# Attention stage of a four-layer block: when a finished group of heads is copied, transposed and divided, and where its products stand

## What is computed

```python
def _L1_ffn_ref(x, attn_norm_w, ffn_norm_w, wq, wk, wv, wo, gate_w, expert_w):
    # _gqa: 16 query heads, 4 key heads, head width 8
    attn = jnp.einsum('bqhd,bkhd->bhqk', q, k) * scale
    attn = jnp.where(causal, attn, jnp.float32(-jnp.inf))
    attn = jax.nn.softmax(attn, axis=-1)
    out = jnp.einsum('bhqk,bkhd->bqhd', attn, v).reshape(B, S, C)
    ...
    h = x + _gqa(_rmsnorm(x, attn_norm_w), wq, wk, wv, wo)
    out = h + _moe(_rmsnorm(h, ffn_norm_w), gate_w, expert_w)   # top 2 of 8 experts
    return out
```

## Time and profile before

| | |
|---|---|
| median of 3 runs | 1509.01 us (1503.67 to 1511.28) |
| the profiled execution | 1498.92 us |
| its span in the trace | 1497.5 us |
| mean granted TensorE clock | 0.892 of full |
| attention steps | from about 846 us to 1464 us of the span |

### The profile page before, as it was taken

The page is one execution under the profiler, slowest core; times in us unless marked ns, Lnnn a source line. Parts: engine busy times, 40 slices in busy tenths (PEclk is TensorE's granted clock), DMA queues, the critical chain, the costliest instruction groups (busy, mean ns, idle before and its releaser), DMA issues. The chain is left out here.

```text
span 1497.5 us, 18717 instructions
## 1 busy us (share of the span) xinstructions
PE 1171.4 (78%) x5568; PEld 540.4 (36%) x5568; DVE 1141.2 (76%) x3062; ACT 734.8 (49%) x1603; POOL 681.7 (46%) x823
## 2 busy tenths in 40 slices
PE   3514997899998877766677778898989889989885
PEld 1202454555545443323221323333333333333222
DVE  5888645757988897888978786787888778778217
ACT  4645684255443344232310457656566456645772
POOL 7433673465777678467550122124421532153312
PEclk9855997999999998887866788999999999999998
DMA  3000104321111100012221301002020302000001
GB/s 110 0 1 0 48 1 109 81 74 64 43 43 43 28 29 0 0 24 46 47 43 39 67 1 37 27 14 39 1 37 4 49 1 37 4 1 1 4 1 56
DMA packets 33682, 47.02 MB, mean 31 GB/s; under 512 B 5023, under 2 KB 18207, under 8 KB 33279
## 3 DMA queue, kind: packets, MB, share of 16 engines
q1 hardware_dynamic: 30990, 43.84, 13.1%
q10 hardware_dynamic: 2592, 2.00, 0.5%
HBM read 39.14 MB, written 6.68 MB: 31 GB/s over the span
## 5 line engine op out<-in xcount | busy, mean ns | idle before, releaser
L1691 ACT ACTIVATE RB<-PS 128x512 f32<-128x512 f32 (+3 forms) x768 | 327.8, 496 | 220.5 <-PE PS L673 216.9
L621 PE MATMUL PS<-B 96*128 96x512 bf16 (+3 forms) x768 | 256.4, 356 | 67.6 <-DVE B L1258 24.1
L1964 POOL TENSOR_SCALAR_AFFINE_SELECT RB<-RB 128x512 f32<-128x512 f32 x128 | 81.3, 635 | 411.5 <-ACT RB L1691 411.5
L1189 DVE CUSTOM_DVE_ANT_0 PS<-PS,w_msk 128x128 f32<-128x128 f32 (+3 forms) x512 | 243.6, 503 | 29.3 <-PE PS L621 28.9
L673 PE MATMUL PS<-B 96*128 96x512 bf16 (+3 forms) x768 | 242.7, 338 | 23.1 <-ACT RB L1691 21.4
L1192 DVE TENSOR_REDUCE SS<-PS 128x1 f32<-128x512 f32 x256 | 175.3, 685 | 44.3 <-PE PS L621 43.2
L690 PE MATMUL PS<-RB,B 128*32 128x512 f32 (+3 forms) x1536 | 171.4, 519 | 14.0 <-ACT RB L1698 14.0
L621 PEld LDWEIGHTS PS<-B 96*128 96x128 bf16 x768 | 77.5, 102 | 218.5 <-DVE SS L1189 67.3
L1870 POOL TENSOR_TENSOR RB<-RB,B 128x512 f32<-128x512 f32 x64 | 82.4, 1290 | 89.0 <-DVE RB L1017 66.8
L673 PEld LDWEIGHTS PS<-B 96*128 96x128 bf16 x768 | 75.6, 100 | 103.5 <-ACT RB L1691 63.9
L1536 ACT ACTIVATE RB<-PS 128x512 f32<-128x512 f32 x72 | 42.8, 596 | 128.4 <-PE PS L438 128.3
(11 more groups left out here) (261 smaller groups left out, 2239.2 us busy)
## 6 DMA issues: line engine op xcount, KB each, us to landing
B<-scrW SPq DMA_DIRECT2D x128, 128.0 KB, 3.0
B<-scrQ SPq DMA_DIRECT2D x72, 128.0 KB
scrQ<-B SPq DMA_DIRECT2D x6, 384.0 KB, 3.0
B<-scrK SPq DMA_DIRECT2D x36, 64.0 KB
X<-in_x SPq DMA_DIRECT2D x8, 256.0 KB, 8.7
out_dram<-X SPq DMA_DIRECT2D x7, 256.0 KB, 3.2
B<-in_w SPq DMA_DIRECT2D x3, 576.0 KB, 5.4
B<-in_zeros SPq DMA_DIRECT2D x9, 128.0 KB
```

What stands on the lines that cost most here:

```text
L621: pe.matmul(p[:, 0:w], qs[u % 3][:, h, 128 * i:128 * i + 128], keys_of(u, h)[:, 512 * c:512 * c + w], start=True, stop=True).then_inc(s["m ...
L1189: ins = dve.tensor_tensor_reduce(p, p, msk[:, 512 - w:512], 1.0, LOWEST, ALU.add, ALU.max, MX[:, u % 2, i, h, c:c + 1])
L1691: act.activation(RB[:, 4 * (step % 3) + z, 0:w], bank(bank_of["score", step, z])[:, 0:w], ACT.Exp).then_inc(s["ex2"], 1)
L1964: pool.affine_select(out=pb, in_=pb, compare_op=ALU.is_ge, fill=0.0, base=0, pattern=[[0, 4], [1, 128]], channel_multiplier=-1).then_inc(s ...
```

## The change

Four things are issued at other places; nothing is added or removed.

- ACT: `sums` stands after the four exps of step E+2, not between the second and third exp of step E+3.
- PE: `heads_2` stays in step E+3, but in front of `product_2(E+1)` instead of behind it.
- DVE: `divide` stands after the four maxima of step E+3, not between the second and third maximum of step E+4.
- PE: the `post_h` slices of every step stand in front of both (behind the scores, ahead of `heads_2` and `product_2`), not at the end of the step. `pass_f(3, k)` of the first unit stays last.

```diff
@@ tensor_program
-                if 0 <= step - PLAG < 192:
-                    product_2(step - PLAG)
+                for g, k in post_slices(step):
+                    post_h(step, g, k)
                 if 0 <= step - PLAG - 1 < 192:
                     n, kt = STEPS[step - PLAG - 1]
                     if kt == 4 * GROUPS[n][2] + 3:
                         heads_2(n)
+                if 0 <= step - PLAG < 192:
+                    product_2(step - PLAG)
                 if u < 7 and r == 20:
                     guard_1(u + 1)
                 for k in late_slices(step):
                     pass_f(3, k, lambda: next_1(step))
-                for g, k in post_slices(step):
-                    post_h(step, g, k)
@@ vector_program
-                for v, n in ahead[0:2]:
+                for v, n in ahead:
                     highest(v, n)
-                if 0 <= step - PLAG - 2 < 192:
-                    n, kt = STEPS[step - PLAG - 2]
+                if 0 <= step - PLAG - 1 < 192:
+                    n, kt = STEPS[step - PLAG - 1]
                     if kt == 4 * GROUPS[n][2] + 3:
                         divide(n)
-                for v, n in ahead[2:]:
-                    highest(v, n)
@@ scalar_program
                 if step < 192:
-                    exps(step, 0)
-                    exps(step, 1)
-                if 0 <= step - PLAG - 1 < 192:
-                    n, kt = STEPS[step - PLAG - 1]
+                    for z in range(4):
+                        exps(step, z)
+                if 0 <= step - PLAG < 192:
+                    n, kt = STEPS[step - PLAG]
                     if kt == 4 * GROUPS[n][2] + 3:
-                        sums(n, step - PLAG - 1)
-                if step < 192:
-                    exps(step, 2)
-                    exps(step, 3)
+                        sums(n, step - PLAG)
```

## The result

The changed kernel took **1454.12 us** (median of 4 runs, 1450.34 to 1458.79) against 1507.42 us for the kernel before (4 runs, 1503.67 to 1511.28). The ratio on record is 0.968, 95% interval 0.9648 to 0.9712; the two medians alone give 0.9646, just outside it. I had forecast 1480 and a range down to 1464. The sign and the places were right; the gain is larger than the range allowed.

A forecast was written before the change was run, and what follows sets the result against it. PE was taken as nearest to the bound, DVE right behind, each waiting in turn at group ends. Terms 4 + 22 + 3 = 29 us off the 1509.0 us median gave 1480 us; the range ran from 1464 to 1505.

The forecast's parts named there:

- Bound and mechanism: Attention stage: PE nearest to a bound, DVE right behind; at group ends they wait in turn, which reordering gives back.
- copy (and transposes): Group ends: copy moved ahead of two exps on ACT, transposes ahead of the product; 4 us won, bounds 0 and 14.
- division: Group ends: division falls into DVE's idle time, so PE's raw blocks stop waiting for it; 22 us won.
- post slices: 28 expert steps: matmuls start a product earlier, mostly off the path; 3 us won, upper bound 5.5, lower a loss.
- worked case: One group end: fourth score at 1096.1 instead of 1095.99, next step's first block 0.1 us earlier.
- The copy holds the exps: Rival: ACT pays the copy's 0.60 us at each of 32 ends on PE's path, 19 us; 1499 us, chance 0.14.
- DVE is the bound: Rival: waits for the division become waits for maxima, copy waits become waits for exps; 1506 us, 3 won, chance 0.11.
- More is won: Rival: all of the load-side wait (34 us) and most of the copy's is won; 1464 us, chance 0.08.
- Slower: Rival: expert matmuls lose their cover and wait for maxima, 22 us, and the clock drops, 20 us; 1525 us, chance 0.05.
- the second rival: The rival that DVE is the bound, 1506 us; chance 0.11, counted as within 0.5% of no change.
- the rest of the first: First rival, the copy holding the exps (chance 0.14): the part beyond the 0.12 counted as faster than 1501.5 us.

The follow-up runs named there:

- e2_copy: Kernel before with only the copy of bank 7 moved, to the end of step E+2 on ACT: 1482.11 us, ratio 0.9888.
- e4_posts_last: The whole change except the post slices, which stay at the end of the step: 1454.25 us, ratio 0.9696 to the kernel before.
- e3_copy_heads: Kernel before with the copy early and the transposes ahead of the product, division and post slices unmoved: 1482.44 us, ratio 0.9884.
- v3_split_norm: The whole change, with ACT's norm of an earlier token group split into two halves, at slices k = 16 and 17: 1442.08 us, ratio 0.9616 to before.
- e6_product_first: The whole change, but with the product kept in front of the transposes: 1465.36 us, ratio 0.9756 to the kernel before.
- e1_divide: Kernel before with only the division moved, to the end of step E+3 on DVE: 1476.90 us, ratio 0.9856.
- v1: The whole change, but post slice k = 0 goes back behind the product: 1454.84 us, ratio 0.9687 to the kernel before.
- e5: Kernel before with only the post slices moved, in front of product and transposes on PE: 1480.60 us, ratio 0.9882.
- v5: The whole change, with ACT's norm of an earlier token group done one tile at each of k = 16 to 19: 1441.80 us, ratio 0.9615 to before.

## Why the prediction was wrong

**Bound and mechanism: right in the main.** PE and DVE had been waiting for each other at the group ends, and DVE could follow. In unit 3 it stood still in 12.2 us of its steps before and in 6.6 after. Every one of the units 1 to 6 became 5.9 to 7.3 us shorter, where I had named 3.5 to 5. What the forecast priced was idle time alone. The stage, before and in the change (columns as in the earlier trace rows):

```profile
834.16:1460.18 626.02, 545.36 (x3444) 213.21 (x3445) 458.93 (x1596) 380.30 (x923) 191.92 (x300) 0.95 0.11 19
```

```profile
836.52:1417.48 580.96, 530.51 (x3445) 209.46 (x3445) 455.95 (x1600) 375.86 (x923) 191.48 (x300) 0.97 0.12 20
```

PE's idle time fell by 30.2 us, from 80.7 to 50.5, and its busy time by 14.9, at a mean clock of 0.95 and then 0.97. Part of the 14.9 is the clock; how the rest splits is not measured.

The stage splits in the order copy and transposes, division, slices (before 626.0, e2_copy 608.1, e4_posts_last 584.2, the change 581.0; e3_copy_heads showed the transposes neutral), and each part into what lies in the three stalls and outside them:

| term | forecast | measured | outside | in the three stalls |
|---|---|---|---|---|
| copy (and transposes) | 4 | 17.9 | 9.6 | 8.3 |
| division | 22 | 23.9 | 18.0 | 5.9 |
| post slices | 3 | 3.2 | 6.4 | -3.2 |
| sum | 29 | 45.0 | 34.0 | 11.0 |

In another order the 11.0 us of the stalls fall to other terms: alone, the slices too give 13.1 us there. Of the 6.4 us of the slices outside, 3.4 are in unit 7, which differs by 2.7 between traces of the change itself.

**Copy and transposes, 4 us: this step failed.** The term measured 17.9 us, and the 13.9 above it are nearly all of the 16 by which the forecast fell short in the stage; 5.6 of them are at the plain ends, 8.3 in the three stalls. It failed twice. At the plain ends I took a value near one worked case, in which two times, the delay of the fourth score and its distance from the product, were assumed and not read. There are four kinds of group end (r = 2, 6, 10, 18), and the one that I worked is the poorest: 0.25 us came back at r = 2, 0.66 at r = 18, where ACT had stood idle before the step. The mean wait of 0.52 us in the list was the better guide; 0.39 of it (1.56 over 4) was won. The list also showed 19.0 us of scores behind exps, more than the 14.0 that I called the next, and I left them out.

**The three stalls** are the other half, 11.0 us in the change, and no term held them. For slice k = 1 I wrote that 0.6 us more of one wait and 0.56 less of another cost nothing net, and did not follow what stood behind. The rows that come after the earlier trace rows in the trace of before:

```profile
1187.14 1.51 PE L715 MATMUL PS<-w_woE,SS 128*128 128x128 f32 x8
...
1188.68 0.69 DVE L1323 TENSOR_TENSOR XA<-XA,PS 128x512 f32<-128x512 f32 x1 [5.37 <-PE PS L715]
...
1191.00 0.39 PE L621 MATMUL PS<-B 96*128 96x512 bf16 x1 [1.86 <-DVE B L1258]
```

The projection (L715) stands third, behind product and transposes, at the low clock; DVE waits 5.37 us for it and adds its result (L1323) ahead of the next maxima and of the division; so the raw block waits 1.86 us for the division and not 1.05 as in the earlier trace rows. The step r = 7 took 4.96, 4.55 and 4.25 us in the three units, and takes 1.76: 8.5 us won, of which my division term priced three times 0.85. r = 8 gives another 1.9 us, where the mean clock had been 0.84, 0.73 and 0.65. But r = 6 itself, the stall that I had in view, gives 0.6 us in three units: 7.49 and 7.28 in unit 4, at 0.77 of the clock both times. By the copy alone it takes 5.25. The change lost that again through its slices, which is the -3.2 of the table; v3_split_norm brings it back.

**Division, 22 us: right in size, in part by luck**: 24.4 alone and 23.9 behind the copy. It took DVE's idle time as forecast, but 6 to 10 us of it are in the three stalls, so at the other ends it gave less than I wrote. That DVE would find the transposes done held in the change, but for three ends, r = 6 of the units 2, 4 and 6, where it waits 2.4 to 3.3 us. With the transposes behind the product there are 26 in all, and e6_product_first gives the price of that order, some 6 us.

**Post slices, 3 us: within what can be told on top of the others** (1.1 to 3.2, mostly in unit 7), although alone they give 18.3, of which 15.1 are PE's busy time (545.4 to 530.3 us in the stage) and only 3.3 idle time. The edits overlap in the stalls and not at the plain ends: in unit 3 the parts alone are 3.6, 1.5 and 0.6, together 5.7, and the whole is 5.9. In the units 2, 4 and 6 they are 10.0, 12.3 and 15.0, together 37.3, and the whole is 21.4.

**The whole time** fell by 48 us in the second and third series (1498.19 less 1450.24, 1498.94 less 1451.25) and by 53 in the first result, over 4 runs. The interval of the recorded ratio holds the 48 and just misses the 53. The traces of the change give 42.9 to 45.1 in the stage; which part of the 53 lay ahead of the stage can't be said, since of the four runs of the kernel before none has a trace.

**Rivals.** *The copy holds the exps* stood beside what the Trainium skill says of ScalarE's queue, that it is taken strictly in order ("TensorE: Matmul & The Clock Gate", "Architectural detail: the array is 16x 32x32, not 1x 128x128"). It is seen at three ends only, r = 5 of the units 2, 4 and 6, 0.64 us each, and as a part of the 1.5 us gap at r = 6; at the others ACT had the time. That a wait of the copy for its product can't be new was wrong: ACT stands there in 9 cases, 9.2 us in the list above (near r = 2, 5 and 17 of the units 2, 4 and 6), and in none of the stage before; yet scores wait only 2.7 us more for exps. *DVE is the bound*: not seen, the waits for maxima grew by 0.7 us. *More is won*, to which I gave 0.08, is what came, though by the copy and the stalls and not by a load-side wait. *Slower*: the expert matmuls do wait more, 8.9 us against 2.2, above all at the first expert step of a token group: r = 22 of the units 3 and 5 takes 5.17 us where it took 4.07. But r = 23 gives 1.04 of it back (3.81 after 4.85), and the mean clock of unit 3 stays at 1.00. In the chances, the second rival and the rest of the first add to 0.13 and not 0.12; the 0.01 stands in the slower case.

## What to carry to other kernels

Where two engines wait for each other in turn, read every kind of place that repeats, and price each by its own rows; a mean wait from the list is a better guide than one worked case in which two times are assumed. Follow a stall to the last engine that stands behind it, and into the step after, before calling an exchange of two waits neutral. Edits that each repair the same stall must be measured together: here they gave 60.6 us one by one and 45 in one kernel.

## What the runs showed of the hardware

The granted clock turned step r = 6 of the units 2, 4 and 6 from 5.3 to 5.9 us into 6.9 to 7.5. It fell more often in the kernels in which PE stood still longer in that step. With 2.08 us (both traces of before, e1_divide) and 1.77 us (the change in all its traces) the mean clock was 0.76 to 0.79 in two of the three units of every trace, and full in the third, from the same code; in e6_product_first, with 1.77, it was low in one (0.80). With 1.51 us (e2, e3, e4, v1) it was low in one of twelve steps, and with 1.08 or less (e5, v3, v5) in none of nine. Step r = 6 alone does not decide it: in e2 and e3, where r = 7 has 1.86 us of idle time, the clock fell in r = 7 in one unit each (0.76 and 0.72) behind an r = 6 at the full level, as in unit 2 of the kernel before (0.74), and in e4 and v1, with 0.02 us or less there, in none. A product of 1.06 us took 1.81 at the lower level, 1.2 GHz. The Trainium skill ("TensorE: Matmul & The Clock Gate", "What's actually happening") says that the clock follows how busy the engine has been; these counts agree.

Most of the scatter that I can place lies ahead of the attention: it began between 830.0 and 844.1 us into the span, in traces of kernels whose code up to there is the same, while unit 3 took 71.9 us in both traces of before and 66.0 in all three of the change. Within the stage, the first unit took 91.0 and 89.9 us in the two traces of before and unit 6 took 83.4 and 84.8; unit 7 took 58.1, 55.5 and 55.5 us in those of the change.
